# Second weights of the looped experts: the low parts subtracted by VectorE and GpSimd, half each

## The chip, the cores and the metric

The kernel runs on one core of one Trainium2 chip. The metric is the device time of one execution in microseconds (us). A core has TensorE (matrix products), VectorE, ScalarE, GpSimd and SyncE; each runs its own list of instructions in order, and they wait for one another through semaphores. In the profile they are PE (PEld is its weight load), DVE, ACT, POOL and SP; a name with q behind it is that engine's sequencer, which reads registers, takes branches and issues DMAs.

## What is computed

A decoder layer in float32 on 4 x 256 tokens of width 256: causal attention of 16 heads and a layer norm, cross attention of 16 heads and a layer norm, then a mixture of 8 experts of which each token uses two. The last part is where the change lies:

```python
x = inputs.reshape(-1, inputs.shape[-1])                       # 1024 tokens in this kernel, D = 256
gate_probs = jax.nn.softmax(x @ gate_w + gate_b, axis=-1)      # E = 8 experts
weights, selected = jax.lax.top_k(gate_probs, K)               # K = 2
...
h = jax.nn.gelu(jnp.einsum('nd,edf->enf', x, w1) + b1[:, None, :])      # F = 1024
expert_out = jnp.einsum('enf,efd->end', h, w2) + b2[:, None, :]
out = jnp.einsum('ne,end->nd', comb, expert_out)
```

and after it `x = _layernorm(x + ffn(x))`.

## The kernel before

The tokens are sorted by expert: GpSimd scatters each token's row to its slots in a table `x_slots` in HBM, and each expert works through its slots in tiles of 128. Experts 0 and 1 have one tile each that is written out ahead of the loops (`EARLY = 2`); then every engine runs a loop over the experts, `for e in range(E)`, and in it a loop over the expert's remaining tiles (`Fori(lo, hi)`), whose bound `hi` each engine reads from memory at run time (`cum_i`). With these inputs 17 tiles run in the loops; experts 2 to 7 have two or three each.

One tile goes through the engines like this:

- TensorE, `h_products`: 32 products (8 blocks of F, 2 chunks of D, each recorded as two) of `w1` with the transposed tokens `xgT`, into four PSUM banks.
- ScalarE, `gelus`: bias and gelu of each block into `hT` (128 x 8 x 128).
- VectorE, `h_splits`: `hT` in three parts (blocks 0 to 2, 3 to 5, 6 and 7). Of each part it copies the rounded high part `hT_hi` and subtracts the low part `hT_lo = hT - hT_hi`. Both read and write SBUF. Then `xgt_evac` copies the next tile's tokens from PSUM.
- TensorE, `y_products`: transposes the next tile's tokens (`xg_transposes`), waits for `w2_split` and for each part of `h_split`, and sums three products for each of the 8 blocks: high x high, high x low, low x high. 24 products in all, lines 608 to 610 of the helper `three`.
- VectorE, `y_add`: adds the bias `b2` into `ys`, once the last store of `ys` has landed. GpSimd then stores `ys` to the table `y_slots` (line 569).

The second weights `w2` are split in the same way once for each expert. ScalarE copies the high part (`w2_high(e + 1)`, in the last tile of expert e), VectorE subtracts the low part (`w2_low(e)`, lines 1607 to 1613) as four instructions of 128 x 512 at the start of expert e, between reading `hi` and the first tile's `h_splits`. Both buffers are double (`e % 2`). A printed name such as `w_lo<-w,w_hi` in the profile is `w2_lo<-w2,w2_hi`: buffer numbers are left out there.

In the last expert GpSimd has one thing more to do: before it stores that expert's tiles it waits for the stores of all the earlier experts (`y_stored`) and issues eight gathers of `y_lo` (line 562). After the last tile it issues eight gathers of `y_hi` (line 574), and the final sum and layer norm follow.

Nothing here is ordered by a planner: each engine's list is the order in which the code is written.

Of the kernel before, what the change touches and what calls it, by code (L numbers as in the profile page):

```python
# [5 lines left out]
def build_decoder_layer(nc, xT_d, x_d, w_attn_d, ctxT_d, w_x_d, qb_d, kb_d, vb_d, ob_d, nq_d, nk_d,  # L6
                        gate_w_d, gate_b_d, w1_d, b1_d, w2_d, b2_d, xs_d, ys_d, out_d):
    f32 = mybir.dt.float32
# [4 lines left out]
    ALU = mybir.AluOpType  # L13
# [20 lines left out]
    FC = F // P  # L34
# [10 lines left out]
    EARLY = 2  # L45

    ctx = ExitStack()
    with ctx:
# [3 lines left out]
        def sb(stack, name, shape, dt=f32):  # L52
# [162 lines left out]
            xs_done xmax_ready xm_done xm_evac xm_in xst_done xexp_done xpv_done z_evac zt_done z_ready zb_done xz_evac  # L215
            xo_done xbias_ready xo_added ln_sums
            x2_ready x2t_done x2t_evac g_in g_done sub_ready gexp_done sel_ready rank_done slots_ready cum_ready
            xs_written xgs_in w_in0 w_in1 b2_in xg_in xgt_done xgt_ready h_done h_gelu h_hi_ready h_split w2_hi_ready w2_split y_done y_evac y_stored
            ylo_in yhi_in0 yhi_in1 yhi_in2 yhi_in3 yhi_in4 yhi_in5 yhi_in6 yhi_in7 var_ready root_ready factors_ready out_ready out_written""".split()
        s = {n: sem(n) for n in names}  # L220

# [157 lines left out]
        def _(pool):  # L379
# [165 lines left out]
            scatter(1)  # L545
            pool.wait_ge(s["xgs_in"], 16 * EARLY)
            scatter(2)
            for e in range(EARLY):
                pool.wait_ge(s["y_evac"], e + 2)
                g.dma_start(ys_d[e * CAP:e * CAP + P, :], ys[:, :]).then_inc(s["y_stored"], 16)  # L550
# [3 lines left out]
            for e in range(E):  # L554
                skip = pool.value_load(first_i[0:1, e:e + 1], min_val=0, max_val=N // P - 1) if e < EARLY else 0
                hi = pool.value_load(cum_i[0:1, e:e + 1], min_val=EARLY + 1, max_val=EARLY + 3 * E)
                if e == E - 1:

                    pool.wait_ge(s["y_stored"], lo * 16 + 16)
                    pool.nop(nofuse=True)  # L560
                    for t in range(TT):
                        g.indirect_dma_start(y_lo[:, t, :], None, ys_d,
                                             bass.IndirectOffsetOnAxis(ap=slot_i[:, t, 0:1], axis=0))\
                            .then_inc(s["ylo_in"], 16)
                with pool.Fori(lo, hi) as i:
                    pool.wait_ge(s["y_evac"], i + 2)
                    row = nc.s_assert_within((i - lo + skip) * P + e * CAP, e * CAP, (e + 1) * CAP - P,
                                             skip_runtime_bounds_check_because="an expert has at most CAP tokens")
                    g.dma_start(ys_d[bass.ds(row, P), :], ys[:, :]).then_inc(s["y_stored"], 16)  # L569
                lo = hi  # L570
# [32 lines left out]
        def _(pe):  # L603
# [341 lines left out]
            def y_products(e, i):  # L945

                xg_transposes(i + 1)
                pe.wait_ge(s["y_evac"], i + 1)
                pe.wait_ge(s["w2_split"], e + 1)
                for f in range(FC):  # L950
                    if f in H_PARTS:
                        pe.wait_ge(s["h_split"], i * NP + NP + 1 + H_PARTS.index(f))
                    last = three(bank[5][:, 0:D], hT_hi[:, f, :], hT_lo[:, f, :], w2_hi[e % 2][:, f, :],
                                 w2_lo[e % 2][:, f, :], f == 0, f == FC - 1)
                last.then_inc(s["y_done"], 1)
# [371 lines left out]
        def _(dve):  # L1327
# [279 lines left out]
            def w2_low(e):  # L1607

                dve.wait_ge(s["w2_hi_ready"], e + 1)
                for f in range(0, FC, 2):  # L1610
                    last = v.tensor_tensor(w2_lo[e % 2][:, f:f + 2, :], w2[e % 2][:, f:f + 2, :],  # L1611
                                           w2_hi[e % 2][:, f:f + 2, :].bitcast(f32), ALU.subtract)
                last.then_inc(s["w2_split"], 1)
# [229 lines left out]
```

## Time and profile before

| | us |
|---|---|
| median of 3 runs | 605.74 (604.71 to 606.5) |
| the profiled execution's own time | 604.01 |
| its span in the trace | 602.3 |
| TensorE busy | 544.7 (90% of the span) |
| VectorE busy | 364.1 (60%) |
| ScalarE busy | 312.8 (52%) |
| GpSimd busy | 169.2 (28%) |

The profiled execution is 1.7 us below the median. Its span leaves 1.7 us of its own time outside (launch and end). The loops over the experts run from 460 us of the span to 580 us. A timeline gives for each instruction its start, its length, the engine, the line of the code and what it writes and reads, and in brackets how long its engine was idle before it and which instruction ended that idle time.

### The profile page before, as it was taken

Reading aid. Unit: us, or ns where it says so; the run is one execution under the profiler, and the core shown is the slowest. Engines: PE = TensorE matmul, PEld = TensorE weight load, DVE = VectorE, ACT = ScalarE, POOL = GpSimd, SP = SyncE. Lnnn points to the kernel's source line nnn. Section 1 sums busy time; section 2 is a strip of 40 time slices with the busy share of each in tenths; the row PEclk is TensorE's granted clock in tenths of the full one; section 3 lists DMA queues with packets and bytes.
Section 4 is the critical chain, followed back from the end, with each engine's and each line's share of the span. In section 5 each row is a group of like instructions: output and inputs, shape, how many; then the busy total and the mean of one; then the engine's idle time right before and its main releaser. Section 6 shows DMA issues by size and latency. Waiting matters only on the chain.

```text
span 602.3 us, 12690 instructions
## 1 busy us (share of the span) xinstructions
PE 544.7 (90%) x3906; PEld 473.5 (79%) x3906; DVE 364.1 (60%) x1142; ACT 312.8 (52%) x856; POOL 169.2 (28%) x280
## 2 busy tenths in 40 slices
PE   2899999999999999999989899998879999999930
PEld 2689989898998989899878566655469999999930
DVE  6075565646556565655576766776586556656545
ACT  1355454545545455454546777755643645545523
POOL 5131212213121231300544689140720100000353
PEclk9999999999999999999999999989989999999985
DMA  8740040502204050182000000020211534444224
GB/s 272 262 185 27 22 172 17 192 17 110 92 24 174 17 192 0 53 344 108 2 2 1 1 2 4 3 72 2 105 53 50 206 148 175 183 177 174 59 80 124
DMA packets 18405, 58.77 MB, mean 98 GB/s; under 512 B 3169, under 2 KB 7521, under 8 KB 13761
## 3 DMA queue, kind: packets, MB, share of 16 engines
q1 hardware_dynamic: 14048, 38.00, 17.4%
q10 hardware_dynamic: 1728, 12.58, 5.4%
q0 software_dynamic: 2592, 7.74, 3.8%
q8 instruction: 19, 0.31, 0.2%
q14 instruction: 18, 0.14, 0.1%
HBM read 35.83 MB, written 22.41 MB: 97 GB/s over the span
## 4 chain that ended last, share of the span: by engine, by line
PE 78%; DVE 9%; issue 4%; POOL 3%; ACT 2%; DMA 2%; DVEq 1%; POOLq 0%; ACTq 0%; SPq 0%
PE bank L608 13%; PE bank L610 13%; PE bank L609 13%; PE bank L941 6%; PE bank L665 5%; PE bank L647 4%; PE bank L655 4%; PE bank L827 3%; PE bank L666 2%; PE bank L646 2%; PE bank L765 2%; PE bank L843 2%; DVE w_lo L1611 2%; PE bank L693 1%; PE bank L787 1%
## 5 line engine op out<-in xcount | busy, mean ns | idle before, releaser
L1298 ACT ACTIVATE hT<-bank,b 128x128 f32<-128x128 f32 x152 | 53.4, 367 | 66.4 <-PE bank L941 63.2
L941 PE MATMUL bank<-xgT,w 128*128 128x128 f32 x608 | 71.7, 276 | 0.5 <-issue 0.5
L941 PEld LDWEIGHTS bank<-xgT,w 128*128 128x128 f32 x608 | 70.0, 193 | 1.0 <-issue 1.0
L608 PE MATMUL bank<-xT_hi,wqk_hi 128*128 128x512 f32 x128 | 56.4, 441 | 11.0 <-DVE wqk_lo L1353 11.0
L1069 ACT ACTIVATE Pr<-Sm,nmax 128x128 f32<-128x128 f32 x64 | 25.8, 403 | 71.1 <-DVE nmax L1362 71.0
L1362 DVE CUSTOM_DVE_ANT_0 Sm<-bank,mask 128x128 f32<-128x128 f32 (+1 forms) x128 | 40.9, 356 | 34.2 <-PE bank L647 34.0
L1497 DVE TENSOR_REDUCE xnmax<-bank 128x2 f32<-128x512 f32 x64 | 43.8, 689 | 24.5 <-PE bank L806 23.6
L610 PE MATMUL bank<-xT_hi,wqk_lo 128*128 128x512 f32 x128 | 51.2, 400 | 0.0
L609 PE MATMUL bank<-xT_lo,wqk_hi 128*128 128x512 f32 x128 | 50.8, 397 | 0.0
L608 PE MATMUL bank<-w_hi,hT_hi 128*128 128x256 f32 x152 | 45.2, 297 | 5.5 <-DVE hT_lo L1624 5.4
L1162 ACT ACTIVATE xPT<-bank 128x512 f32<-128x512 f32 x64 | 37.6, 596 | 19.5 <-PE bank L827 19.2
L1384 DVE TENSOR_TENSOR z_lo<-bank,z_hi 128x256 fp32r<-128x256 f32 x64 | 27.2, 424 | 32.8 <-ACT z_hi L1062 32.4
L1378 DVE TENSOR_TENSOR acc<-acc,bank 128x256 f32<-128x256 f32 x64 | 26.9, 421 | 29.9 <-PE bank L610 29.7
L610 PE MATMUL bank<-w_hi,hT_lo 128*128 128x256 f32 x152 | 43.6, 287 | 0.0
L609 PE MATMUL bank<-w_lo,hT_hi 128*128 128x256 f32 x152 | 43.5, 286 | 0.0
L1062 ACT ACTIVATE z_hi<-bank 128x256 fp32r<-128x256 f32 x64 | 24.6, 384 | 34.8 <-PE bank L666 33.7
L608 PE MATMUL bank<-wo_hi,z_hi 128*128 128x256 f32 x128 | 42.6, 333 | 0.0
L608 PE MATMUL bank<-wv_hi,xT_hi 128*128 128x256 f32 x128 | 39.0, 305 | 2.6 <-ACT V L1057 2.6
L665 PE MATMUL bank<-PT,V 128*128 128x256 f32 x128 | 38.7, 384 | 1.8 <-DVE z_lo L1384 1.8
L647 PE MATMUL bank<-KT,QT 128*128 128x256 f32 x128 | 38.2, 381 | 0.0
L569 POOL DMA_DIRECT2D y_slots<-ys x17 | 9.4, 553 | 98.0 <-DVE ys L1631 98.0
L610 PE MATMUL bank<-wv_hi,xT_lo 128*128 128x256 f32 x128 | 36.2, 283 | 0.0
(244 smaller groups left out, 1510.2 us busy)
## 6 DMA issues: line engine op xcount, KB each, us to landing
w<-in_w ACTq DMA_DIRECT2D x12, 1024.0 KB, 6.3
w_raw<-in_w_attn SPq DMA_DIRECT2D x32, 256.0 KB, 3.6
x_slots<-w SPq DMA_DIRECT2D x8, 1024.0 KB, 5.5
y_slots<-w SPq DMA_DIRECT2D x7, 1024.0 KB, 7.4
w<-in_w SPq DMA_DIRECT2D x4, 1024.0 KB, 7.8
y_slots<-ys POOLq DMA_DIRECT2D x19, 128.0 KB, 2.1
xg<-x_slots SPq DMA_DIRECT2D x18, 128.0 KB, 2.1
xT_raw<-in_xT SPq DMA_DIRECT2D x2, 512.0 KB, 5.6
```

The lines of the kernel that those rows point to most:

```text
L608: mm(out, lh, rh, start=start, stop=False)
L609: mm(out, lh, rl, start=False, stop=False)
L610: return mm(out, ll, rh, start=False, stop=stop)
L647: mm(ps[:, P:P + S], q_[:, at + P:at + S], k_[:, at:at + S], start=True, stop=True)\
L665: mm(ps_z[:, 0:S], V[:, 2 * b, hh * DH:(hh + 1) * DH], PT[st % 2][:, 0:S], start=True, stop=False)
L941: last = mm(ps_h[f % 4][:, 0:P], w1[e % 2][:, c, f * P:(f + 1) * P], xgT[:, c, :], start=c == 0, stop=c == DC - 1)
L1162: A(xPT[j % 8][:, :, :], ps_xt[j % 2][:, :].rearrange("p (a n) -> p a n", a=2), ACT.Exp)\
L1298: A(hT[:, f, :], ps_h[f % 4][:, 0:P], ACT.Gelu_apprx_tanh, bias=b1[:, e, f:f + 1])\
L1362: last = v.tensor_tensor_reduce(out=Sm[buf][:, a:z], in0=ps_s[buf][:, a:z], in1=mask[:, a:z], scale=1.0, scalar=BIG, op0=ALU.add, op1=ALU.min,
L1378: v.tensor_tensor(acc[:, t, :], acc[:, t, :], o_bank(p, t)[:, 0:D], ALU.add).then_inc(s["o_added"], 1)
L1384: v.tensor_tensor(z_lo[:, hh, cols], ps_z[:, 0:S], z_hi[:, hh, cols].bitcast(f32), ALU.subtract)\
L1497: v.tensor_reduce(xnmax[u % 2][:, at:at + 2], ps_s[i % 2][:, :].rearrange("p (a n) -> p a n", a=2), AX.X, ALU.max, negate=True).then_inc(s ...
```

## The change

For the experts of the loops from number 2 on, VectorE subtracts blocks 0 to 3 of F (two instructions of 128 x 512 in place of four), and GpSimd gets a function `w2_low` of its own that subtracts blocks 4 to 7 (two instructions of the same shape), called after it has read `hi` and before its loop over the tiles. In the last expert that is also before the gathers of `y_lo`. GpSimd signals a new semaphore, `w2_split_pool`. TensorE waits for VectorE's half where it waited before, and for GpSimd's half ahead of block 4. The wait stands in `y_products`, so each tile of the expert has it; after the first tile it is satisfied already. Experts 0 and 1 are left as they were.

```diff
+            def w2_low(e):
+
+                pool.wait_ge(s["w2_hi_ready"], e + 1)
+                for f in range(FC // 2, FC, 2):
+                    last = g.tensor_tensor(w2_lo[e % 2][:, f:f + 2, :], w2[e % 2][:, f:f + 2, :],
+                                           w2_hi[e % 2][:, f:f + 2, :].bitcast(f32), ALU.subtract)
+                last.then_inc(s["w2_split_pool"], 1)
...
                 hi = pool.value_load(cum_i[0:1, e:e + 1], min_val=EARLY + 1, max_val=EARLY + 3 * E)
+                if e >= EARLY:
+                    w2_low(e)
                 if e == E - 1:
...
                 for f in range(FC):
+                    if f == FC // 2 and e >= EARLY:
+                        pe.wait_ge(s["w2_split_pool"], e + 1 - EARLY)
                     if f in H_PARTS:
...
                 dve.wait_ge(s["w2_hi_ready"], e + 1)
-                for f in range(0, FC, 2):
+                for f in range(0, FC if e < EARLY else FC // 2, 2):
                     last = v.tensor_tensor(w2_lo[e % 2][:, f:f + 2, :], w2[e % 2][:, f:f + 2, :],
                                            w2_hi[e % 2][:, f:f + 2, :].bitcast(f32), ALU.subtract)
```

GpSimd's list at the last expert, from the store of expert 6's last tile to the gathers of `y_lo`, before (the two rows of ISA behind the load are the register work and the bound's check):

```order
L569 DMA y_slots<-ys 128x256
L565 REGISTER_ALU
L565 COMPARE_AND_BRANCH
L556 TENSOR_LOAD cum_i
L556 ISA x2
L559 ISA
L562 DMA y_lo<-y_slots,slot_i 128x256 [waits y_stored]
L562 DMA y_lo<-y_slots,slot_i 128x256 x7
```

and in the changed kernel:

```order
L579 DMA y_slots<-ys 128x256
L575 REGISTER_ALU
L575 COMPARE_AND_BRANCH
L564 TENSOR_LOAD cum_i
L564 ISA x2
L552 TENSOR_TENSOR w_lo<-w_1,w_hi 128x512 [waits w2_hi_ready]
L552 TENSOR_TENSOR w_lo<-w_1,w_hi 128x512
L569 ISA
L572 DMA y_lo<-y_slots,slot_i 128x256 [waits y_stored]
L572 DMA y_lo<-y_slots,slot_i 128x256 x7
```

The two subtractions stand back to back, with no wait between them, behind the store and ahead of the gathers. In experts 2 to 6 they stand at the same place, with the loop over the tiles behind them.

TensorE's list inside `y_products` of an expert from number 2 on, blocks 3 and 4, before:

```order
L952 REGISTER_ALU
L608 MATMUL bank<-w_hi,hT_hi 128x256 [waits h_split]
L609 MATMUL bank<-w_lo,hT_hi 128x256
L610 MATMUL bank<-w_hi,hT_lo 128x256
L608 MATMUL bank<-w_hi,hT_hi 128x256
L609 MATMUL bank<-w_lo,hT_hi 128x256
```

and in the changed kernel:

```order
L964 REGISTER_ALU
L618 MATMUL bank<-w_hi,hT_hi 128x256 [waits h_split]
L619 MATMUL bank<-w_lo,hT_hi 128x256
L620 MATMUL bank<-w_hi,hT_lo 128x256
L618 MATMUL bank<-w_hi,hT_hi 128x256 [waits w2_split_pool]
L619 MATMUL bank<-w_lo,hT_hi 128x256
```

No product moved; the first of block 4 has a wait of its own.

## Rows read from the trace of the kernel before

**Rows 1.** Page: busy us and share of PE; shares of the chain that ended last.

```profile
PE 544.7 (90%) x3906; PEld 473.5 (79%) x3906; DVE 364.1 (60%) x1142; ACT 312.8 (52%) x856; POOL 169.2 (28%) x280
...
PE 78%; DVE 9%; issue 4%; POOL 3%; ACT 2%; DMA 2%; DVEq 1%; POOLq 0%; ACTq 0%; SPq 0%
```

**Rows 2.** Timeline of PE, expert 2: start, us, engine, line, operation, [idle before <- releaser].

```profile
482.45 0.38 PE L930 MATMUL bank<-ident,xg 128*128 128x128 f32 x2
483.38 0.39 PE L608 MATMUL bank<-w_hi,hT_hi 128*128 128x256 f32 x1 [0.55 <-DVE hT_lo L1624]
...
486.36 3.73 PE L941 MATMUL bank<-xgT,w 128*128 128x128 f32 x32
489.93 0.38 PE L930 MATMUL bank<-ident,xg 128*128 128x128 f32 x2
493.01 3.73 PE L941 MATMUL bank<-xgT,w 128*128 128x128 f32 x32
```

**Rows 3.** Timelines of DVE and ACT at the start of expert 2.

```profile
479.16 0.42 DVE L1631 TENSOR_TENSOR ys<-bank,b 128x256 f32<-128x256 f32 x1 [1.69 <-PE bank L610]
479.97 2.50 DVE L1611 TENSOR_TENSOR w_lo<-w,w_hi 128x512 fp32r<-128x512 f32 x4 [0.38 <-issue]
482.38 0.36 DVE L1622 CAST hT_hi<-hT 128x384 fp32r<-128x384 f32 x1
482.77 0.56 DVE L1624 TENSOR_TENSOR hT_lo<-hT,hT_hi 128x384 fp32r<-128x384 f32 x1
...
480.14 1.98 ACT L1298 ACTIVATE hT<-bank,b 128x128 f32<-128x128 f32 x6 [1.72 <-PE bank L941]
```

**Rows 4.** POOL: the store ahead of expert 2, line 428's group, line 556's last part.

```profile
480.27 0.54 POOL L569 DMA_DIRECT2D y_slots<-ys  x1 [5.29 <-DVE ys L1631]
...
L428 POOL TENSOR_TENSOR wv_lo<-w_raw,wv_hi 128x512 fp32r<-128x512 f32 x7 | 8.9, 1274 | 0.6
...
L556 POOLq SEQ_ASSERT  x8: 18/18/24, 462.3 to 565.1; - x8
```

**Rows 5.** Timelines of POOL and DVE where both work in SBUF.

```profile
5.33 1.91 POOL L411 MEMSET Vd<- 128x512 f32 x4
7.19 0.55 POOL L413 MEMSET stack_k<- 128x256 f32 x2
...
5.38 2.65 DVE L1347 CAST xT_hi<-xT_raw 128x512 fp32r<-128x512 f32 x1 [4.32 <-DMA xT_raw<-in_xT]
...
8.67 0.42 DVE L1347 CAST xT_hi<-xT_raw 128x512 fp32r<-128x512 f32 x1
...
323.57 0.49 DVE L1457 SCALAR_TENSOR_TENSOR qn<-q_tok,qrs,rows_bc 128x256 f32<-128x256 f32 x1
...
325.30 0.84 DVE L1457 SCALAR_TENSOR_TENSOR qn<-q_tok,qrs,rows_bc 128x256 f32<-128x256 f32 x1
...
325.07 0.79 POOL L480 TENSOR_TENSOR stack_k<-kn,stack_k 128x256 fp32r<-128x256 f32 x1
```

**Rows 6.** PE after two idle stretches; windows (us, PE busy, granted clock, DMA share, GB/s).

```profile
315.50 0.73 PE L665 MATMUL bank<-PT,V 128*128 128x256 f32 x1 [1.80 <-DVE z_lo L1384]
...
447.34 0.36 PE L608 MATMUL bank<-w_hi,hT_hi 128*128 128x256 f32 x1 [1.89 <-DVE hT_lo L1624]
...
448.00:450.00 2.00, 2.00 (x14) 0.67 0.22 78
450.00:452.00 2.00, 2.00 (x12) 0.50 0.18 66
```

**Rows 7.** POOL and DVE around the gathers of the last expert.

```profile
564.50 0.54 POOL L569 DMA_DIRECT2D y_slots<-ys  x1 [6.11 <-DVE ys L1631]
567.35 1.09 POOL L562 DMA_INDIRECT y_lo<-y_slots,slot_i  x1 [2.32 <-DMA y_slots<-ys]
...
577.68 0.58 POOL L569 DMA_DIRECT2D y_slots<-ys  x1
...
579.87 0.42 DVE L1631 TENSOR_TENSOR ys<-bank,b 128x256 f32<-128x256 f32 x1 [3.93 <-DMA y_slots<-ys]
```

More of the change, by code:

```diff
@@ L217, in build_decoder_layer @@
             x2_ready x2t_done x2t_evac g_in g_done sub_ready gexp_done sel_ready rank_done slots_ready cum_ready
-            xs_written xgs_in w_in0 w_in1 b2_in xg_in xgt_done xgt_ready h_done h_gelu h_hi_ready h_split w2_hi_ready w2_split y_done y_evac y_stored
+            xs_written xgs_in w_in0 w_in1 b2_in xg_in xgt_done xgt_ready h_done h_gelu h_hi_ready h_split w2_hi_ready w2_split w2_split_pool y_done y_evac y_stored
             ylo_in yhi_in0 yhi_in1 yhi_in2 yhi_in3 yhi_in4 yhi_in5 yhi_in6 yhi_in7 var_ready root_ready factors_ready out_ready out_written""".split()
```

## The prediction, made before the changed kernel ran

> **What bounds the kernel now.** I read the page first: TensorE is busy for 90% of the span and makes 78% of the chain that ended last [rows 1]. So only what stands between two products counts, and I went to the timelines of the place that the change touches, the first tile of an expert. In expert 2 TensorE starts the next tile's transposes at 482.45 and its next `h_products` at 486.36, 3.91 us later; in the tile after it, which has no subtraction ahead, the same stretch takes 493.01 - 489.93 = 3.08 us [rows 2]. The first tile costs 0.83 us more, and the row on line 608 says why: TensorE waits for VectorE's `hT_lo`. The same holds in experts 2 to 6, between 0.83 and 0.96 us each, about 4.3 us in all. VectorE is late since the four subtractions of `w2_low` hold it for 2.50 us from 479.97, and the tile's `hT_hi` can only follow at 482.38 [rows 3].
>
> The last expert is bound by something else. There GpSimd issues its gathers of `y_lo` from 567.35 to 577.68, only then stores `ys`, and VectorE's last `ys` waits 3.93 us for that store to land [rows 7]. TensorE's time in that expert is covered, and GpSimd's is not.
>
> **The change, part by part.**
>
> *VectorE loses two of four subtractions.* Four take 2.50 us, so one takes about 0.61, and the two that are left end near 481.25. ScalarE's six gelus run from 480.14 for 1.98 us [rows 3], so the third, for which `hT_hi` waits, ends near 481.15. `hT_hi` can start at 481.27 in place of 482.38, `hT_lo` takes 0.39 + 0.56 more and ends at 482.2, ahead of the transposes' end (482.83). Undisturbed, TensorE would wait for nothing: a gain of 4.3 us over five experts.
>
> *GpSimd gains two subtractions of 128 x 512.* The nearest row is the same operation on the same shape in the attention stage, 1.274 us each, so 2.55 us for the two [rows 4]. When do they start? In the last expert the store starts at 564.50 and the check of `hi` at 565.1 [rows 4, 7]: 0.6 us, and 0.1 until the engine starts. In expert 2 the store starts at 480.27 [rows 4], so the subtractions start near 480.97 and end near 483.5 if nothing hinders them. TensorE needs block 4 twelve products after its start (0.12 us each, from 24 products in some 2.9 us), at 484.05 at the earliest. The new wait on TensorE has half a microsecond of cover. With it lost, whatever GpSimd is late would be added one for one to each first tile, since all the later products and the next tile stand behind it on TensorE.
>
> *The two engines then work in SBUF at the same time, and this trace shows what that costs.* VectorE's cast at 5.38 takes 2.65 us; the same cast takes 0.42 at 8.67. Beside it GpSimd runs six memsets back to back, from 5.33 to 7.19 + 0.55 = 7.74, and the cast ends at 8.03, 0.29 after them [rows 5]: VectorE waited through all six. With GpSimd reading two tensors it is the same: VectorE's operation at 325.30 takes 0.84 where its like took 0.49 at 323.57, and it ends at 326.14, 0.28 after GpSimd's `TENSOR_TENSOR` (325.07 + 0.79 = 325.86) [rows 5]. Both kinds are what `h_splits` is made of: a cast from SBUF to SBUF, and a subtraction with both inputs in SBUF.
>
> Put into expert 2: GpSimd asks at 480.97, while VectorE's second subtraction runs until 481.25, and is next in line. VectorE's `hT_hi` asks at 481.27, behind it. GpSimd holds on for 2.55 us until 483.8; `hT_hi` ends 0.25 later, at 484.05, `hT_lo` after 0.56 more, at 484.6. Line 608 starts at 484.6 in place of 483.38: the first tile gets 1.2 us longer than it is now, not 0.83 shorter. GpSimd's signal (483.8) comes ahead of block 4 anyway. Nor is it of use if GpSimd comes a little late and `hT_hi` slips in first: `hT_lo` then waits for the same end. Over five experts that is 5 x 1.2 = 6.0 us. Bounds: 0.9 each if VectorE gets in between the two subtractions, 1.3 if GpSimd starts a little later, so 4.5 to 6.5.
>
> The Trainium skill says of this (SBUF — State Buffer, "Who interferes with whom") that VectorE and GpSimd share one pair of ports, that an operation of VectorE with two SBUF inputs contends with GpSimd's reads, as does one that runs in a two-port mode, and that the second to issue stands still until the first has finished. The trace agrees, with 0.84 for 0.49. The page gives the pair for one instruction at a time, though, while the cast at 5.38 waited through six.
>
> *TensorE's clock.* The new wait leaves TensorE idle from 482.83 to 484.6, 1.77 us. Two idle stretches of nearly that length stand in this trace, 1.80 and 1.89 us [rows 6], and behind each the granted clock falls to half. Behind the second the rows show 0.67 and 0.50 of full speed in two windows of 2 us [rows 6], that is 2 x 0.33 + 2 x 0.50 = 1.7 us of TensorE's time, of which some 1.5 is lost on products that would otherwise follow each other at 0.12. The 0.55 of now [rows 2] is followed by no drop. So each of the five first tiles may cost 1.5 us more. I take two of the five, not all, since 1.77 is just short of both that are known: 3.0 us. Bounds: 0 and 7.5.
>
> *The last expert.* GpSimd's two subtractions stand ahead of the gathers. In the trace of before it idles 2.32 us there until its store has landed [rows 7], so part of them is covered: they start at 565.2, get the port at 565.4, end at 568.0, and the first gather starts at 568.0 to 568.4 in place of 567.35. From there the chain is GpSimd's to the end. I take 0.8 us, bounds 0.5 and 1.3. TensorE's extra 1.2 us in that expert is covered: the last `ys` waits 3.93 us for the store.
>
> *Covered or free:* the new semaphore's wait in later tiles (satisfied), GpSimd's stores of first tiles (they come 4 us after its subtractions), the weight loads on ScalarE's queue.
>
> **Sum** against the profiled execution: 604.0 + 6.0 + 3.0 + 0.8 = 613.8. The median is 1.7 above that execution, so 605.7 + 9.8 = 615.5 us.
>
> **The rivals.**
>
> 1. *The ports block VectorE, but the clock stays full.* For it: one idle stretch here is 1.77 and the two known are longer. Against: by little. 605.7 + 6.0 + 0.8 = 612.5. The Trainium skill speaks for this one (TensorE: Matmul & The Clock Gate, the summary's row on throughput drops): it asks for a longer idle stretch than either of the two that the trace shows ahead of a drop.
> 2. *The ports change hands between GpSimd's two subtractions.* Then VectorE's `hT_hi`, or both of its first operations, run between them, and TensorE loses 0.45 (it waits for the second part of `h_split` only) to 1.07 us a first tile, with idle stretches too short for the clock: 5 x 0.45 to 5 x 1.07, and 0.8: 608.8 to 611.9, say 610.5. The Trainium skill's rule above, taken word for word, gives this one. Against it: the six memsets.
> 3. *On the other side: the two engines get on.* If the two subtractions don't stop `h_splits`, the wait of 0.83 us goes in five experts, 4.3 us less, and the last expert gives 0.5 back: 602.0. It decides at the start of `hT_hi`: this case needs GpSimd's port to be free at 481.27. For it: products of VectorE with one input in PSUM run beside GpSimd unhindered. Against: rows 5, and none of `h_splits` reads PSUM.
> 4. *Nothing to measure.* The block costs about what the shorter list gains, 0 to 0.3 a first tile: 605.7.
>
> **How the numbers follow.** Forecast (ports and clock) 0.45; rival 1 0.20; rival 2 0.17; rival 3 0.13; rival 4 0.05. The likeliest is the forecast, 615.5; its own range goes with one to four drops, 613 to 619.5. The whole range is to reach rivals 1 and 2 as well and leaves out 3 and 4 (0.18): 607.5 to 619.5. About 0.3% (1.8 us) is what a measurement of this kernel can tell from no change. Slower by more than that: 0.45 + 0.20 + 0.17 = 0.82. Faster: 0.13. Within: 0.05.
>
> **What the profile after would show.** For the ports: in experts 2 to 7 a `hT_hi` of 2.5 us or more (0.36 now) whose end lies just behind GpSimd's second subtraction, and line 608 of first tiles idle for some 1.8 us behind `hT_lo`. For the clock: windows behind them at half. For the last expert: the first gather 0.7 to 1.0 us later behind its store than the 2.85 of now. For rival 2: a `hT_hi` of about 1.5 us between the two. For rival 3: `hT_hi` at 0.36, no idle ahead of line 608. The forecast is wrong if GpSimd starts its work so late that VectorE is through with the first part, or if VectorE's operations go first when both wait.

## The result, and the profile after

| | before | after |
|---|---|---|
| median of 11 runs each, same chip | 604.71 us (602.96 to 606.50) | 609.36 us (607.74 to 617.09) |
| ratio, with its 95% interval | | 1.0087 [1.0064, 1.0110] |
| profiled execution, its span | 604.01, 602.3 | 611.22, 609.5 |
| from the first `ys` to the last `ys` of expert 6 | 111.6 us | 115.3 us |
| last store ahead of the gathers to the first gather | 2.85 us | 3.61 us |

The changed kernel is slower by 5.3 us (3.9 to 6.7 by the interval; one run of the eleven, 617.09 us at a granted clock of 0.953 where the others have 0.970 to 0.976, isn't in the ratio). That is the forecast sign and inside the range of 607.5 to 619.5, but below the forecast's own range of 613 to 619.5, and about half of the forecast 9.8 us. The medians alone differ by 4.65 us. The two profiled executions lie further apart (7.2 us) than the medians, and the last two rows of the table account for 3.7 + 0.8 = 4.5 us of it; the rest is from stages that the change doesn't touch (2.1 us ahead of the first `ys`, 0.7 behind the last).

The page of after, the same lines as [rows 1]: busy time and share, and the chain that ended last.

```profile
PE 546.4 (90%) x3906; PEld 474.7 (78%) x3906; DVE 369.0 (61%) x1130; ACT 312.9 (51%) x856; POOL 185.3 (30%) x292
...
PE 77%; DVE 10%; issue 4%; POOL 3%; DMA 2%; ACT 2%; DVEq 1%; POOLq 0%; SPq 0%; ACTq 0%
```

VectorE has twelve instructions less than in [rows 1] (1130 for 1142) and is busy 4.9 us longer. That alone says that something stretches what it has kept. GpSimd gained twelve and 16 us.

The timeline of DVE at the start of expert 2, after, the stretch of [rows 3] (start, us, engine, line, operation, idle time before and its releaser):

```profile
480.98 0.42 DVE L1643 TENSOR_TENSOR ys<-bank,b 128x256 f32<-128x256 f32 x1 [1.69 <-PE bank L620]
481.81 1.29 DVE L1623 TENSOR_TENSOR w_lo<-w,w_hi 128x512 fp32r<-128x512 f32 x2 [0.40 <-issue]
483.02 1.43 DVE L1634 CAST hT_hi<-hT 128x384 fp32r<-128x384 f32 x1
484.48 1.50 DVE L1636 TENSOR_TENSOR hT_lo<-hT,hT_hi 128x384 fp32r<-128x384 f32 x1
485.90 0.35 DVE L1634 CAST hT_hi<-hT 128x384 fp32r<-128x384 f32 x1
486.28 0.56 DVE L1636 TENSOR_TENSOR hT_lo<-hT,hT_hi 128x384 fp32r<-128x384 f32 x1
```

and of POOL and PE beside it:

```profile
482.10 0.54 POOL L579 DMA_DIRECT2D y_slots<-ys  x1 [5.26 <-DVE ys L1643]
482.85 2.72 POOL L552 TENSOR_TENSOR w_lo<-w,w_hi 128x512 fp32r<-128x512 f32 x2 [0.21 <-issue]
...
484.28 0.38 PE L940 MATMUL bank<-ident,xg 128*128 128x128 f32 x2
486.03 0.39 PE L618 MATMUL bank<-w_hi,hT_hi 128*128 128x256 f32 x1 [1.37 <-DVE hT_lo L1636]
```

The two subtractions left on VectorE take 1.29 us in place of 2.50 [rows 3]: 1.21 gained. Then the cast takes 1.43 in place of 0.36 and the subtraction behind it 1.50 in place of 0.56 [rows 3]: 1.07 + 0.94 = 2.01 lost. The balance, 0.80 us, is about what TensorE waits longer: 1.37 for 0.55 [rows 2]. GpSimd's pair runs from 482.85 to 485.57. The cast ends at 484.45, inside it, and the next subtraction at 485.98, 0.41 behind it. So VectorE was not held through the pair: it waited for the first of GpSimd's subtractions (which ends at 484.23), ran its cast, waited for the second, and ran its subtraction. GpSimd waits too: each of its twelve subtractions ends 1.12 or 1.13 us behind the end of the VectorE instruction that was running when it began. Experts 2 to 7 all show this, with casts of 1.43, subtractions of 1.50 and idle stretches of 1.36 to 1.40. From `ys` to `ys` such a tile takes 8.32 us, 7.50 before.

The granted clock behind that stretch (windows: us, busy time of the five engines, clock, DMA share, GB/s):

```profile
486.00:488.00 2.00, 1.97 (x16) 1.97 (x17) 1.77 (x5) 0.00 (x0) 0.00 (x0) 1.00 0.95 394
488.00:490.00 2.00, 2.00 (x19) 2.00 (x18) 0.42 (x1) 0.27 (x1) 0.00 (x0) 1.00 0.14 49
```

It stays at full speed, behind all six. TensorE never waits for `w2_split_pool`: no group of the trace names GpSimd's `w_lo` as a releaser of PE.

The last expert, POOL, where [rows 7] stand before:

```profile
570.23 0.55 POOL L579 DMA_DIRECT2D y_slots<-ys  x1 [6.10 <-DVE ys L1643]
570.98 2.71 POOL L552 TENSOR_TENSOR w_lo<-w,w_hi 128x512 fp32r<-128x512 f32 x2 [0.20 <-issue]
573.84 1.16 POOL L572 DMA_INDIRECT y_lo<-y_slots,slot_i  x1 [0.15 <-issue]
```

The first gather starts 3.61 us behind the store; it waits for the subtractions and no longer for the store to land.

### The profile page after: what moved, and what is told of

The parts are those of the page before. It is cut to its first block, busy times and chain, and to the rows that moved or that the text cites. A ratio compares the mean times of both kernels' runs of the same rounds, so it can differ in the third digit from the quotient of the medians.

```text
span 609.5 us, 12690 instructions
## 1 busy us (share of the span) xinstructions
PE 546.4 (90%) x3906; PEld 474.7 (78%) x3906; DVE 369.0 (61%) x1130; ACT 312.9 (51%) x856; POOL 185.3 (30%) x292
## 4 chain that ended last, share of the span: by engine, by line
PE 77%; DVE 10%; issue 4%; POOL 3%; DMA 2%; ACT 2%; DVEq 1%; POOLq 0%; SPq 0%; ACTq 0%
PE bank L618 13%; PE bank L620 13%; PE bank L619 13%; PE bank L951 6%; PE bank L675 5%; PE bank L657 4%; PE bank L665 4%; PE bank L837 3%; PE bank L676 2%; PE bank L775 2%; PE bank L656 2%; PE bank L853 2%; DVE hT_lo L1636 2%; DVE hT_hi L1634 2%; PE bank L797 1%
## 5 line engine op out<-in xcount | busy, mean ns | idle before, releaser
L618 PEld LDWEIGHTS bank<-w_hi,hT_hi 128*128 128x128 f32 x152 | 29.8, 196 | 12.1 <-DVE hT_lo L1636 10.0
L426 POOL CAST wqk_hi<-w_raw 128x512 fp32r<-128x512 f32 x14 | 8.5, 609 | 97.3 <-PE bank L620 88.5
```

The lines of the kernel that those rows point to most:

```text
L618: mm(out, lh, rh, start=start, stop=False)
```

## The experiments

Eleven runs in three groups, each on a chip of its own. Kernels of one group ran on the same chip and are compared only with the kernel before on that chip (604.54 us in the first group, 613.45 in the second, 613.15 in the third). Edits are against the changed kernel, but for e4_ahead and e8_ahead. "Loops" is the time from the first `ys` to the last `ys` of expert 6 in the trace of each, as the difference from a trace of before: 111.6 for the first two groups, which have no trace of before from their own chip, 111.4 for the third, from b0_before. "Gather" is store to first gather, against 2.85.

| | median | ratio [95%] | loops | gather | idle of TensorE, first tiles |
|---|---|---|---|---|---|
| e0_after | 608.86 | 1.0075 [1.0027, 1.0123] | +3.7 | +0.77 | 1.36 to 1.40 |
| e1_half_only | 601.24 | 0.9958 [0.9916, 0.9999] | -4.2 | 0 | none |
| e2_one_long | 607.43 | 1.0055 [1.0013, 1.0096] | +4.5 | +0.51 | 1.50 to 1.54 |
| e3_four_short | 607.74 | 1.0058 [1.0017, 1.0099] | +1.7 | +1.50 | up to 0.32 ahead of block 0, 0.48 to 0.50 ahead of block 3 |
| e5_last_dve | 617.11 | 1.0064 [1.0033, 1.0094] | +3.8 | 0 | 1.36 to 1.38, last 0.58 |
| e6_memset | 610.18 | 0.9960 [0.9939, 0.9982] | -3.1 | +0.77 | none; once 0.66; last 1.39 |
| e4_ahead | 612.28 | 0.9974 [0.9952, 0.9997] | -3.5 | +0.32 | none, but 0.37 in expert 3's second tile; last 0.57 |
| e8_ahead (the same kernel) | 610.16 | 0.9956 [0.9932, 0.9981] | -3.5 | +0.30 | none, but 0.39 in expert 3's second tile; last 0.57 |
| e7_five_blocks | 628.17 | 1.0242 [1.0207, 1.0277] | +13.0 | +1.04 | 1.94 to 2.04, last 1.68 |
| e9_after | 618.81 | 1.0102 [1.0070, 1.0134] | +4.0 | +0.75 | 1.36 to 1.40 |
| b0_before | 612.62 | 0.9992 [0.9965, 1.0018] | 0 | 0 | 0.55 to 0.68 |

**The changed kernel again, and the kernel before again.** e0_after and e9_after are the changed kernel in the first and the third group, b0_before is the kernel before in the third, for a trace of it there.

> The changed kernel itself again, as the ground for the three beside it. Theory P (one pair of ports, held for one instruction of GpSimd at a time, so VectorE gets in between the two subtractions): hT_hi of a first tile takes about 1.43 us, hT_lo 1.50, TensorE is idle for 1.37 ahead of line 618, and the time is that of before plus 4.2 (five tiles at 0.83) plus 0.8 (gathers) = plus 5 us. A rival W (TensorE's new wait or GpSimd's late signal costs the time) expects TensorE to be released by w2_split_pool somewhere; P expects that never.

> The changed kernel on this chip: before plus 5 us (five first tiles at 0.83 and the gathers at 0.8), first tiles with an idle stretch of 1.37 us and no fall of the clock behind any of them.

> The kernel before the change itself, for a trace beside the next three on the same chip. Theory S (on some chips the last tile of the last expert is slow whatever the kernel, since TensorE and ScalarE stand still there for reasons outside their lists): its last y_add comes 11 to 14 us behind the one before it, where the trace of before has 8.99. Rival: it is 9.0, and what was seen with e4, e5 and e6 comes from their edits.

The loops and the gathers give +4.5 and +4.7 us, and the measured ratios 4.5 (1.6 to 7.4) and 6.3 (4.3 to 8.2). In e9_after's trace the last tile of the loops is 1.3 us longer than in b0_before's, of which more at the end. The twelve idle stretches lie between 1.36 and 1.40 us, and no fall of the clock follows any of them. The kernel before gave 0.9992 against itself.

**Is VectorE's shorter list worth what the prediction says, and is the rest GpSimd's doing?** e1_half_only leaves out GpSimd's two subtractions and the wait for them, so the low parts of blocks 4 to 7 of `w2` are not computed in experts 2 to 7.

```diff
                 hi = pool.value_load(cum_i[0:1, e:e + 1], min_val=EARLY + 1, max_val=EARLY + 3 * E)
-                if e >= EARLY:
-                    w2_low(e)
...
-                    if f == FC // 2 and e >= EARLY:
-                        pe.wait_ge(s["w2_split_pool"], e + 1 - EARLY)
```

> VectorE's part of the change alone: it subtracts the first half only, GpSimd does nothing, TensorE has no second wait, so the low parts of blocks 4 to 7 are left out (they keep the values of experts 0 and 1). All theories that put the whole loss on GpSimd's work expect the relief in full: no wait of TensorE in first tiles, hT_hi 0.36 us, before minus 4.3 us. If it is clearly less, shortening VectorE's list is worth less than the 0.83 to 0.96 us a first tile that the prediction took, and part of the miss sits there.

DVE and PE at the start of expert 2:

```profile
480.79 1.29 DVE L1619 TENSOR_TENSOR w_lo<-w,w_hi 128x512 fp32r<-128x512 f32 x2 [0.40 <-issue]
482.00 0.35 DVE L1630 CAST hT_hi<-hT 128x384 fp32r<-128x384 f32 x1
482.38 0.56 DVE L1632 TENSOR_TENSOR hT_lo<-hT,hT_hi 128x384 fp32r<-128x384 f32 x1
...
483.26 0.38 PE L938 MATMUL bank<-ident,xg 128*128 128x128 f32 x2
483.39 0.36 PE L616 MATMUL bank<-w_hi,hT_hi 128*128 128x256 f32 x1
```

The cast is back at 0.35, and line 616 follows the transposes with no idle time before it. The loops lose 4.2 us, as the prediction had it (4.3); by the ratio the kernel is 2.5 us faster (0.1 to 5.1), by the medians 3.3. So the relief is real, and what takes it away, and as much again, comes with GpSimd's two instructions.

**Does the port change hands after each of GpSimd's instructions?** The forecast said that VectorE is held through all that GpSimd does back to back, rival 2 that it gets in between. The same elements in one instruction or in four tell them apart: under the forecast the number of instructions changes nothing, under rival 2 one instruction holds the cast for its whole length and lets the next subtraction run free, and four hold four operations of VectorE, each for a short time.

```diff
-                for f in range(FC // 2, FC, 2):
-                    last = g.tensor_tensor(w2_lo[e % 2][:, f:f + 2, :], w2[e % 2][:, f:f + 2, :],
-                                           w2_hi[e % 2][:, f:f + 2, :].bitcast(f32), ALU.subtract)
-                last.then_inc(s["w2_split_pool"], 1)
+                h = slice(FC // 2, FC)
+                g.tensor_tensor(w2_lo[e % 2][:, h, :], w2[e % 2][:, h, :], w2_hi[e % 2][:, h, :].bitcast(f32),
+                                ALU.subtract).then_inc(s["w2_split_pool"], 1)
```

> The changed kernel with GpSimd's half as one instruction of 128x1024 in place of two of 128x512: the same work with no seam. P: VectorE can't get in, hT_hi of a first tile takes 2.5 to 2.7 us, hT_lo then its usual 0.56, line 618 starts 1.2 us later than before the change and TensorE is idle for about 1.75 us: before plus 6.8 us. If an idle stretch of 1.75 lowers the granted clock, 1.5 us more for each of the five in which it does, up to 14. The rival H (what costs is the number of hand-overs, not the length of an instruction) expects one hand-over less, so less than the changed kernel: before plus 2 to 4.

POOL and DVE at the start of expert 2, one long instruction:

```profile
479.28 2.47 POOL L552 TENSOR_TENSOR w_lo<-w,w_hi 128x1024 fp32r<-128x1024 f32 x1 [0.21 <-issue]
...
479.45 2.51 DVE L1633 CAST hT_hi<-hT 128x384 fp32r<-128x384 f32 x1
481.99 0.56 DVE L1635 TENSOR_TENSOR hT_lo<-hT,hT_hi 128x384 fp32r<-128x384 f32 x1
```

```diff
-                for f in range(FC // 2, FC, 2):
-                    last = g.tensor_tensor(w2_lo[e % 2][:, f:f + 2, :], w2[e % 2][:, f:f + 2, :],
-                                           w2_hi[e % 2][:, f:f + 2, :].bitcast(f32), ALU.subtract)
+                for f in range(FC // 2, FC):
+                    last = g.tensor_tensor(w2_lo[e % 2][:, f, :], w2[e % 2][:, f, :],
+                                           w2_hi[e % 2][:, f, :].bitcast(f32), ALU.subtract)
```

> The changed kernel with GpSimd's half as four instructions of 128x256 (0.72 us each by the attention stage's rows). P: hT_hi waits for the first only, hT_lo for the second, so hT_hi takes about 0.95 us, hT_lo 1.0, line 618 starts where it did before the change or 0.1 us sooner; GpSimd's last part then ends about when block 4 needs it. Five tiles at minus 0.1 to plus 0.3, the gathers plus 1.0 to 1.5: before plus 0.5 to 3 us. H expects four hand-overs and more than the changed kernel: before plus 7 or more.

POOL and DVE at the start of expert 2, four short ones, and PE, which now waits twice:

```profile
481.44 3.46 POOL L552 TENSOR_TENSOR w_lo<-w,w_hi 128x256 fp32r<-128x256 f32 x4 [0.21 <-issue]
...
481.61 0.88 DVE L1634 CAST hT_hi<-hT 128x384 fp32r<-128x384 f32 x1
482.53 0.97 DVE L1636 TENSOR_TENSOR hT_lo<-hT,hT_hi 128x384 fp32r<-128x384 f32 x1
483.42 0.88 DVE L1634 CAST hT_hi<-hT 128x384 fp32r<-128x384 f32 x1
484.34 0.98 DVE L1636 TENSOR_TENSOR hT_lo<-hT,hT_hi 128x384 fp32r<-128x384 f32 x1
...
483.55 0.39 PE L618 MATMUL bank<-w_hi,hT_hi 128*128 128x256 f32 x1 [0.30 <-DVE hT_lo L1636]
485.37 0.39 PE L618 MATMUL bank<-w_hi,hT_hi 128*128 128x256 f32 x1 [0.48 <-DVE hT_lo L1636]
```

Rival 2's pattern, in three forms. One instruction: the cast waits through all of it (2.51, ending at 481.96, 0.21 behind GpSimd's end at 481.75) and the subtraction isn't held (0.56). Two: one operation waits for each. Four: four operations wait, 0.4 to 0.5 us each, and the fifth, the 128 x 256 cast, is free again. It is one operation of VectorE for one of GpSimd. The order doesn't matter: in expert 4 the cast came first and ran in 0.35, and the next four operations were held. GpSimd pays too. Whatever VectorE instruction still runs when a GpSimd subtraction begins, the subtraction ends a fixed time behind that one's end: 1.12 or 1.13 us for all 46 of 128 x 512 in after, e0, e5 and e9, 0.58 to 0.60 for the 24 of 128 x 256 in e3, 2.21 or 2.22 for the six of 128 x 1024 in e2.

TensorE pays 0.95 us more than before in a first tile with one long instruction, 0.82 with two, and about 0.4 on average over the five with four, where the delay falls partly on the second part of `h_split`, which TensorE needs later. In the last expert the order is the other way round, since the gathers stand behind the whole chain: +0.51, +0.77, +1.50 us. Over the kernel the three can't be told apart by time (1.0055, 1.0075, 1.0058); the rows tell them apart. e3's own expectation (0.5 to 3 us) had only the first two operations held; four are, and the traces' 1.7 + 1.5 = 3.2 us is the result.

e2 was expected to lose the forecast's 1.2 us a tile, whether the port is handed over or not, and 6.8 us in all. It lost 0.95 a tile and 3.3 us in all by the ratio (0.8 to 5.8; 5.0 by its rows). By time alone it fits rival H of the expectations, that the number of hand-overs is what costs (2 to 4); against H stand the rows, 0.95 a tile with one instruction and 0.82 with two, and e3, for which H had 7 or more and 3.5 (1.0 to 6.0) was measured. Why 0.95 and not 1.2: GpSimd ends 3.22 us behind the start of its store (478.53 to 481.75), where the working had 3.53 (480.27 to 483.8). The long instruction takes 2.47 us with 0.25 of VectorE's second subtraction still to run, and 2.35 in expert 5 with 0.13, where two were put at 2.55 with 0.28 of waiting on top.

**How much is the last expert's?** e5_last_dve leaves all four subtractions of expert 7 to VectorE.

```diff
-                if e >= EARLY:
+                if EARLY <= e < E - 1:
                     w2_low(e)
...
-                    if f == FC // 2 and e >= EARLY:
+                    if f == FC // 2 and EARLY <= e < E - 1:
...
-                for f in range(0, FC if e < EARLY else FC // 2, 2):
+                for f in range(0, FC if e < EARLY or e == E - 1 else FC // 2, 2):
```

> The changed kernel with the last expert's four subtractions given back to VectorE. The first gather comes 2.85 us behind its store again, not 3.61: the changed kernel minus 0.8 us, so before plus 4.2. If the last expert's part costs nothing at the end (the gathers' delay is absorbed by the final stage), before plus 5 as the changed kernel.

```profile
574.64 0.55 POOL L579 DMA_DIRECT2D y_slots<-ys  x1 [6.10 <-DVE ys L1643]
577.52 1.09 POOL L572 DMA_INDIRECT y_lo<-y_slots,slot_i  x1 [2.34 <-DMA y_slots<-ys]
```

2.88 us again from store to gather, and expert 7's idle stretch is 0.58. The loops' +3.8 is left, and the ratio gives 3.9 us (2.0 to 5.8). The trace shows the gathers' 0.76 us plainly; the timing doesn't resolve so small a part.

**Was the row of the six memsets the wrong one to read?** In experts 2 to 6, e6_memset lets GpSimd write zeros in five back-to-back memsets of 128 x 512 into buffers that are overwritten later, in place of the subtractions; the low parts of blocks 4 to 7 of those experts are not computed. Expert 7 keeps its real subtractions.

```diff
             def w2_low(e):
+                if e < E - 1:
+                    if e > EARLY:
+                        pool.wait_ge(s["w2_split_pool"], e - EARLY)
+                    for part in (y_hi[:, 0:2, :], y_hi[:, 2:4, :], y_hi[:, 4:6, :], y_hi[:, 6:8, :], y_lo[:, 0:2, :]):
+                        last = g.memset(part, 0.0)
+                    last.then_inc(s["w2_split_pool"], 1)
+                    return
```

> The changed kernel, but in experts 2 to 6 GpSimd writes zeros (five memsets of 128x512 back to back, 0.51 us each, 2.57 in all, into y_hi and y_lo, which the gathers fill later) in place of subtracting; the low parts of blocks 4 to 7 are left out there. GpSimd is as long at work and reads nothing. If only reads collide, h_splits runs free and the time is before minus 4.3 plus 0.8 = minus 3.5 us. If a cast of VectorE from SBUF to SBUF collides with writes too, as at the kernel's start, hT_hi waits: through all five (2.5 us, as there), and the time is about before plus 6 or more; or for one only (0.5 us), and it is about before minus 3. hT_lo is expected at 0.56 either way.

POOL and DVE in expert 2, then in expert 5:

```profile
489.06 2.34 POOL L555 MEMSET y_hi<- 128x512 f32 x4 [0.17 <-issue]
...
489.26 0.53 DVE L1641 CAST hT_hi<-hT 128x384 fp32r<-128x384 f32 x1
489.83 0.56 DVE L1643 TENSOR_TENSOR hT_lo<-hT,hT_hi 128x384 fp32r<-128x384 f32 x1
490.31 0.63 DVE L1641 CAST hT_hi<-hT 128x384 fp32r<-128x384 f32 x1
...
535.93 2.13 POOL L555 MEMSET y_hi<- 128x512 f32 x4 [0.26 <-issue]
538.01 0.52 POOL L555 MEMSET y_lo<- 128x512 f32 x1
...
537.18 1.57 DVE L1641 CAST hT_hi<-hT 128x384 fp32r<-128x384 f32 x1
```

Beside memsets a cast mostly takes 0.53 to 0.65 us: it gets in between two of them. A subtraction with both inputs in SBUF takes 0.56 as if alone. A memset behind such a cast takes 0.73 for 0.52. Twice a cast was passed over: in expert 5 it took 1.57 us and ended 0.22 behind the last memset, so it had waited through three, and in expert 4 one of 128 x 256 (0.29 alone) took 1.00 and waited through the last two. The cast at 5.38 of [rows 5] is thus not a freak, but it isn't the rule either, and no such case appears beside the subtractions. What decides it stays open. The kernel is faster than before by 2.4 us (1.1 to 3.7); its loops gain 3.1 and its gathers lose 0.8: without reads by GpSimd most of the relief stays. In expert 7 of this same run the real subtractions give 1.43, 1.50 and an idle stretch of 1.39 again.

**Was the clock step right in kind?** e7_five_blocks leaves VectorE blocks 0 to 2, gives GpSimd blocks 3 to 7 in one instruction and makes TensorE wait ahead of block 3, so that the idle stretch passes the two known ones (1.80 and 1.89).

```diff
-                for f in range(FC // 2, FC, 2):
...
+                h = slice(3, FC)
+                g.tensor_tensor(w2_lo[e % 2][:, h, :], w2[e % 2][:, h, :], w2_hi[e % 2][:, h, :].bitcast(f32),
+                                ALU.subtract).then_inc(s["w2_split_pool"], 1)
...
-                    if f == FC // 2 and e >= EARLY:
+                    if f == 3 and e >= EARLY:
```

> The changed kernel, but VectorE subtracts blocks 0 to 2 and GpSimd blocks 3 to 7 in one instruction of 128x1280, and TensorE waits for it ahead of block 3. P: by 2.46 us for 1024 columns, GpSimd holds the ports for about 3.05 us, hT_hi of a first tile takes 3.0 to 3.4 us, and TensorE is idle for 1.9 to 2.0 us: the stretch that the other traces have once, at 1.89, and behind which the granted clock fell in six of nine. So before plus 5 x 1.4 plus about 1.2 = plus 8, and, if such a stretch lowers the clock in about half of the cases, 1.5 us for each of some three: plus 12 to 13. If the clock doesn't fall, plus 8.

Its profiled execution took 634.57 us, the five others 624.79 to 628.89: its clock stood at half for 27 us from 401 on, ahead of the loops, where the other traces have 0 to 7 us. So only the rows of the first tiles and the clock behind them are read from it. Expert 3, DVE and PE, and the windows behind:

```profile
515.68 3.00 DVE L1635 CAST hT_hi<-hT 128x384 fp32r<-128x384 f32 x1
...
519.32 0.39 PE L617 MATMUL bank<-w_hi,hT_hi 128*128 128x256 f32 x1 [1.96 <-DVE hT_lo L1637]
...
520.00:522.00 2.00, 2.00 (x14) 2.00 (x13) 1.09 (x4) 0.00 (x0) 0.00 (x0) 0.63 0.51 193
522.00:524.00 2.00, 2.00 (x11) 2.00 (x11) 0.00 (x1) 0.00 (x0) 0.00 (x0) 0.51 0.01 4
```

The clock falls from 2.4 to 1.2 GHz behind four of the six stretches, those of experts 3 to 6. A first tile takes 8.88 us without a fall (expert 2) and 10.19 to 10.46 with one: 1.4 us for a fall, or 1.5 with the tile behind it counted, as in the prediction. Five tiles of 1.38 more, four falls of 1.5 and 1.0 for the gathers are 13.9 us; the ratio gives 14.8 (12.7 to 17.0). The five other executions have a mean granted clock of 0.960 or 0.961, and b0_before's 0.966 to 0.974.

How sure is a fall? The two stretches of [rows 6], 1.80 and 1.89 us, lie in code that no kernel here changes, so every trace repeats them. Over the twelve traces other than e7's, a fall follows the first in 7 (before, after, e1, e2, e6, b0, e9) and the second in 7 (before, after, e1, e3, e4, e6, e9). In e0_after neither is followed by one:

```profile
444.40 0.36 PE L618 MATMUL bank<-w_hi,hT_hi 128*128 128x256 f32 x1 [1.89 <-DVE hT_lo L1636]
...
444.00:446.00 2.00, 1.60 (x13) 1.63 (x14) 1.93 (x6) 0.00 (x0) 1.39 (x3) 1.00 0.18 66
446.00:448.00 2.00, 2.00 (x19) 2.00 (x18) 2.00 (x5) 0.01 (x1) 0.76 (x1) 1.00 0.37 131
```

Two of two in the trace of before was chance on a matter of 14 in 24. None of the 24 stretches of 1.36 to 1.40 us in first tiles of after, e0, e5, e6 and e9, nor of the six of 1.50 to 1.54 in e2, is followed by a fall. But the length of one stretch doesn't decide alone. In nine of all thirteen traces the clock also falls near 401 us, behind an idle stretch of 0.79, and in six near 343 us, behind two of 0.85; in the last tile of e6 it falls behind one of 1.42. In the trace of before (PE, and two windows):

```profile
399.48 0.50 PE L806 MATMUL bank<-XK,QS 64*128 64x256 f32 x2 [0.78 <-DVE xnmax L1497]
...
400.00:402.00 2.00, 1.89 (x18) 0.71 (x18) 1.89 (x5) 0.47 (x1) 1.47 (x7) 0.72 0.04 9
402.00:404.00 2.00, 2.00 (x14) 1.44 (x12) 0.69 (x1) 0.98 (x2) 0.99 (x5) 0.50 0.00 0
```

That row was there to be read before the run: the two stretches of [rows 6] were neither sure to bring a fall nor the only places that have one. What decides stays open. The Trainium skill (TensorE: Matmul & The Clock Gate, the summary's row on throughput drops) asks for a longer idle stretch than any of these before a drop; the stretches of 0.79 to 2.04 us with a fall behind them speak against it here.

**A version that beats both.** e4_ahead leaves GpSimd out, as in the kernel before, and takes VectorE's subtractions from the first tile's path: for experts 2 to 6 it does them in the last tile of the expert before, between that tile's `xgt_evac` and its `ys`. For that the body of the loop is turned, so that a tile's `ys` comes ahead of the next tile's splits. Expert 7 is treated as before. This edit is against the kernel before; the waits of `y_add` are moved by one tile to fit.

```diff
...
-                if e >= EARLY:
+                if e == E - 1:
                     w2_low(e)
-                with dve.Fori(lo, hi) as i:
-                    h_splits(i)
-                    xgt_evac(i + 3)
-                    y_add(e, i)
+                if EARLY <= e + 1 < E - 1:
+                    h_splits(lo)
+                    xgt_evac(lo + 3)
+                    with dve.Fori(lo + 1, hi) as i:
+                        y_add(e, i, 0)
+                        h_splits(i)
+                        xgt_evac(i + 3)
+                    w2_low(e + 1)
+                    y_add(e, hi, 0)
...
```

> The kernel before the change, with VectorE alone and all four subtractions, but those of experts 2 to 6 stand ahead of the last y_add of the expert before (VectorE is idle there for 1.7 us, waiting for TensorE); the last expert's stay where they were. If the loss of 0.83 us a first tile is VectorE's lateness, it goes without GpSimd: y_add ends near 481.3 in the frame of the trace of before, hT_hi follows at once, hT_lo ends at 482.3: before minus 4 us (minus 3 to minus 4.3). If y_add being 1.8 us late costs something (the store of ys, which the next y_add waits for, lands later under the weight loads), the gain is smaller, 0 to minus 2.

> The kernel of e4 again: VectorE's subtractions of experts 2 to 6 ahead of the last y_add of the expert before. Between the last tile of expert 1 and the last of expert 6 the trace of e4 had 79.3 us where before has 84.2. If that is worth its time at the end: before minus 4 us. If the last tiles of the last expert give it back, as in e4: before minus 1.

DVE around the start of expert 2 in e8_ahead:

```profile
484.05 2.50 DVE L1611 TENSOR_TENSOR w_lo<-w,w_hi 128x512 fp32r<-128x512 f32 x4 [0.99 <-ACT w_hi L1189]
486.46 0.42 DVE L1631 TENSOR_TENSOR ys<-bank,b 128x256 f32<-128x256 f32 x1
486.80 0.35 DVE L1622 CAST hT_hi<-hT 128x384 fp32r<-128x384 f32 x1
487.18 0.56 DVE L1624 TENSOR_TENSOR hT_lo<-hT,hT_hi 128x384 fp32r<-128x384 f32 x1
```

The four subtractions now stand where VectorE waited for the products before (1.69 us idle ahead of `ys` in [rows 3]). They hold that `ys` up a little, but TensorE doesn't wait for it, and the cast at 486.80 follows `ys` directly. Once it costs something: in expert 3's second tile `ys` waits 4.40 us for the late store to land, and TensorE then 0.39 for `hT_lo`. The time is 0.9974 [0.9952, 0.9997] and 0.9956 [0.9932, 0.9981] of before, 1.6 (0.2 to 2.9) and 2.7 us (1.2 to 4.2); the loops give 3.5 in both, less 0.3 for the gathers. The expectations had 4 in the main case; both are short of it. Against the changed kernel on the same chip it is 610.16 to 618.81 us. e4 showed most of its gain gone in the last tile (14.10 us from `ys` to `ys`), which led to b0_before: there the kernel before takes 11.68 on that tile (8.99 in the first trace of it), and e8_ahead 11.68 too. So the edit doesn't slow the last tile on that chip. On e4's chip, where e5 and e6 take 11.83 and 11.53, the other 2.3 us of e4's 14.10 go with a fall of the clock inside that tile; whether the edit has a part in it, no run shows.

## Where the prediction was right, and the steps that failed

*Right.* **The relief**: 0.83 to 0.96 us a first tile if nothing hinders; e1 has 4.2 us over the loops. **The mechanism in kind**: the cast and the subtraction of `h_splits` are held while GpSimd subtracts in SBUF, and this costs more than the shorter list gives; e1 and e6, without GpSimd's subtractions in experts 2 to 6, are both faster than before. **The new wait is free**: TensorE never waits for it. **The last expert**: 0.8 us forecast, 0.76 in the trace, 0 in e5 where GpSimd has nothing to do there.

*Wrong: TensorE's clock, 3.0 us put down and 0 measured.* The step is "I take two of the five", behind idle stretches of 1.77 us. In the changed kernel the stretches are 1.36 to 1.40 and nothing falls behind any of them. Handing over isn't the main reason: in e2, where VectorE is held from end to end as the forecast had it, they are 1.50 to 1.54, and nothing falls either. So the stretch was put too long, and that a fall follows 1.77 rested on two stretches in one trace; over twelve traces it is 14 of 24 for 1.80 and 1.89. The price of a fall held (1.4 to 1.5 measured, 1.5 forecast), and e7 shows that with stretches of 1.94 to 2.04 falls come. What stretches of 1.77 would do, no run shows: the nearest are e7's last, 1.68 with no fall behind it, and those of 1.80.

*Wrong: how long VectorE is held, 6.0 us put down and 4.1 measured.* The step is "GpSimd holds on for 2.55 us until 483.8", and it fails twice. First in length, by 0.25 us a tile: held from end to end, e2's first tiles lose 0.95 and not 1.2, since 1024 columns on GpSimd end 2.22 us behind VectorE's last subtraction and not 2.55. Adding two rows of 1.274 [rows 4], and the wait on top, was too much. Then in kind, by another 0.13: VectorE gets in between the two, and the tile loses 0.82. This rested on the cast at 5.38 that waited through six memsets [rows 5]. The rows around 325.30 were nearer in kind and show the alternation. With [rows 5], from the trace of before, POOL and DVE:

```profile
324.25 0.74 POOL L479 CAST stack_k<-kn 128x512 fp32r<-128x512 f32 x1 [5.22 <-PE bank L765]
...
324.56 0.71 DVE L1462 TENSOR_TENSOR stack_q<-qn,stack_q 128x256 fp32r<-128x256 f32 x1
```

GpSimd's cast ends at 324.99 and VectorE's subtraction 0.28 behind it, at 325.27 (0.71 us for 0.42 at 326.80). GpSimd's `TENSOR_TENSOR` at 325.07 ends at 325.86, 0.59 behind that, as the instructions of its shape do in e3; VectorE's operation at 325.30 ends 0.28 behind that again. Each waited for one of the other. The operations behind these, of other kinds, don't show it as clearly. The Trainium skill (SBUF — State Buffer, "Who interferes with whom") gives the pair for one instruction, and e0, e2 and e3 agree for reads, with 1.43 and 1.50, 2.51 and 0.56, 0.88 and 0.97. The prediction had this as rival 2, with 0.45 to 1.07 a tile, and gave it 0.17. In the trace of after the first tiles and the ones behind them give 3.9 us (0.79 to 0.82 in four experts, 0.67 in expert 5).

*The sum with the measured terms:* 4.1 + 0 + 0.8 = 4.9 us, against 5.3 (3.9 to 6.7) by the ratio. The forecast started from 605.7, the median of three runs; the eleven runs have 604.7, which gives 609.6 for the 609.36 measured. The range held since it had been drawn down to rival 2, not by the forecast's own mechanism.

## What to carry to other kernels

Work moved from VectorE to GpSimd was not free here, since VectorE's own operations at that time were casts from SBUF to SBUF and subtractions with two inputs in SBUF. Where that is so, count, for each GpSimd instruction that reads SBUF, one VectorE operation that waits for it, and see who waits for that operation. If the work isn't urgent, another time on the same engine can be better than another engine: the last tile of the expert before had room for VectorE's subtractions. A behaviour seen once or twice in one trace, be it a held port or a fall of the clock, deserves a chance and not a certainty, and between two rows the one with the same kind of operation weighs more than the one with the longer effect. Look also for the same behaviour where the explanation doesn't expect it: the falls near 401 us stood in the trace of before.

## What the runs showed of the hardware that was not expected

- The handing over of the port is one for one. VectorE's operation waits for the GpSimd instruction that runs, GpSimd's next one waits for that operation: 1.43 and 1.50 us beside two of 1.37, 2.51 then 0.56 beside one of 2.47, four of 0.88 to 0.98 beside four that took 3.46 together. GpSimd's subtractions end 0.59, 1.12 and 2.22 us (256, 512 and 1024 columns) behind the VectorE instruction that they met.
- Beside memsets the casts are mostly held for one at a time (0.53 to 0.65), but once for two (1.00 for 0.29), once for three (1.57), and at the start of the kernel for six [rows 5]; subtractions are not held at all (0.56).
- Idle stretches of 1.80 and 1.89 us of TensorE were followed by a fall of the granted clock to half in 14 of 24 cases, stretches of 1.94 to 2.04 in four of five, the first tiles' stretches of 1.36 to 1.54 in none of 30. Yet nine of thirteen traces have a fall behind a stretch of 0.79 at 401 us. One fall costs 1.4 to 1.5 us here.
- In the second and third group the last tile of the last expert took 11.5 to 14.1 us from `ys` to `ys`, in the kernel before as well, where the first group and the traces of before and after have 8.5 to 9.7. In b0_before TensorE waits there for ScalarE's gelus, whose releaser the trace gives as `remote`, no instruction of this core:

```profile
586.36 1.14 ACT L1298 ACTIVATE hT<-bank,b 128x128 f32<-128x128 f32 x4 [2.39 <-remote]
588.02 0.39 PE L608 MATMUL bank<-w_hi,hT_hi 128*128 128x256 f32 x1 [2.01 <-DVE hT_lo L1624]
```

The same traces have another such wait ahead of the loops, in which TensorE is idle near 430 us for 4.7 to 4.9 us (3.1 in e7) behind ScalarE's `zt`; in b0_before its releaser is `remote` too. The two make up most of the 8.6 us between the first chip of the experiments and the third. Their cause stays open.
